# Top-32 attention: no fourth replacement; kept keys found again by signs and a triangle product

## The chip, the cores and the metric

One NeuronCore of one Trainium2 chip runs the whole program. The metric is the device time of one execution in microseconds. The program is a four-layer decoder of twelve sublayers; the change lies in one of them, the self-attention of the last layer.

## The reference, cut to what matters

For each of 8 sequences of 256 tokens and each of 16 heads of 8 features, a query keeps the 32 keys with the highest scores, takes the softmax over these, and mixes their values. Of equal scores the lower key index is kept, since that is how `top_k` orders them.

```python
scores = jnp.einsum('bhsd,bhtd->bhst', q, k) / scale
top_s, top_i = jax.lax.top_k(scores, 32)
probs = jax.nn.softmax(top_s, axis=-1)
v_g = gather(v, top_i)
out = jnp.einsum('bhsk,bhskd->bhsd', probs, v_g)
out = out.transpose(0, 2, 1, 3).reshape(b, s, e)
return out @ Wo.T + bo
```

## The kernel before, in words

`topk_attention` works on 64 groups, one after the other. A group is two heads of one sequence: four tiles (`U = 4`, head by half of the queries) of 128 queries x 256 keys. Two groups share a projected tile of queries and keys, so 32 tiles. Each engine has its own in-order program, and semaphores join them. Nothing is scheduled by a tool: the loops over `t` at the end of each engine's block give the order.

For group n, TensorE writes scores into two PSUM banks (`score`, L3552; two pairs of banks take turns). VectorE (`choose`, L3696 and L3699) then works four rounds: in a round `max` finds the eight highest of each tile, and `match_replace` overwrites exactly these eight (first places first, so ties go right) in the copy `raw`. After four rounds `raw` lacks exactly the 32 kept keys. ScalarE (`soften`) sums the exponentials of the 32 maxima (L3641) and takes exponentials of the scores (L3645) and of `raw` (L3647), whose replaced places give 0. GpSimd (`pick`) subtracts the two (L3747), which leaves the kept keys alone, and multiplies by the inverse sum (L3749). TensorE transposes (`turn`, L3598), ScalarE copies (`take_turned`, L3656), TensorE mixes with the values (`mix`, L3575), ScalarE copies the heads (`take_heads`, L3664). `project` (L3539, L3540) and `take_queries` (L3629, L3630) come once for two groups; `put_out`, `take_output` and `add` once for eight.

Of the kernel before, what the change touches and what calls it, by code (L numbers as in the profile page):

```python
# [70 lines left out]
class Core:  # L71
# [19 lines left out]
        "biases_placed", "mask_spread",  # L91
# [3403 lines left out]
def topk_attention(c):  # L3495
# [6 lines left out]
    NG, GROUPS, TILES = H // 2, B * H // 2, B * H // 4  # L3502
    a = Arena(c)
    qb, kb = a.take(2, S), a.take(2, S)
    probs, rest, raw = a.take(2, U, S), a.take(2, U, S), a.take(2, U, S)
# [3 lines left out]
    nbias, sums, rsum = a.take(2, U), a.take(2, U), a.take(2, U)  # L3509
    top8, few = a.take(2, U, K // 8, 8), a.take(2, U, K)  # L3510
    values = c.T[:, 0, :].rearrange("p (t f) -> p t f", f=P)
# [6 lines left out]
    def scores(n):  # L3518
        return c.psum[:, 2 * (n % 2):2 * (n % 2) + 2, :].rearrange("p a (q k) -> p (a q) k", k=S)
# [10 lines left out]
    with nc.Block() as block:  # L3530
        @block.tensor
        def _(pe):
# [10 lines left out]
            def score(n):  # L3543
                tile = n // 2
                if n % 2 == 0:
                    pe.wait_ge(c.qk_taken.sem, c.qk_taken.at(tile + 1))
                if n >= 2:
                    pe.wait_ge(c.probs_ready.sem, c.probs_ready.at(n - 1))
                for u in range(U):
                    lo = (n % 2 * 2 + u // 2) * 32  # L3550
                    head = slice(lo, lo + 32)
                    mm = nc.tensor.matmul(scores(n)[:, u, :], qb[head, tile % 2, u % 2 * P:(u % 2 + 1) * P],  # L3552
                                          kb[head, tile % 2, :], start=True, stop=True, tile_position=(lo, 0))
                mm.then_inc(c.scores_ready.sem, 1)
# [9 lines left out]

            def mix(n):
                b, tile = n // NG, n // 2
                pe.wait_ge(c.turned_copied.sem, c.turned_copied.at(n + 1))
                if n == 0:
                    pe.wait_ge(c.v_taken.sem, c.v_taken.at(4))
# [18 lines left out]
            def turn(n):  # L3588
                pe.wait_ge(c.probs_picked.sem, c.probs_picked.at(n + 1))
                if n == 0:  # L3590
                    pe.wait_ge(c.v_taken.sem, c.v_taken.at(4))
                else:
                    pe.wait_ge(c.turned_copied.sem, c.turned_copied.at(n))
                for head in range(2):
                    for kt in range(2):
                        for q in range(2):
                            at = (kt * 2 + q) * P
                            mm = nc.tensor.transpose(bank(4 + head)[:, at:at + P],  # L3598
                                                     probs[:, n % 2, 2 * head + q, kt * P:(kt + 1) * P], ident)
                mm.then_inc(c.probs_turned.sem, 1)  # L3600
# [6 lines left out]
            for t in range(GROUPS + 3):  # L3607
                if t + 1 < GROUPS:
                    score(t + 1)
                if t % 2 == 0 and t // 2 + 1 < TILES:  # L3610
                    project(t // 2 + 1)
# [6 lines left out]
                if 0 <= t - 1 < GROUPS:  # L3618
                    turn(t - 1)

        @block.scalar
        def _(act):
            ch = Chain(act, c.scalar_chain)

            def take_queries(tile):
                act.wait_ge(c.qk_ready.sem, c.qk_ready.at(tile + 1))
                if tile >= 2:
                    act.wait_ge(c.scores_ready.sem, c.scores_ready.at(2 * tile - 2))
                nc.scalar.activation(kb[:, tile % 2, :], bank(7)[:, 0:S], ACT.Identity, bias=bk[:, tile % 4:tile % 4 + 1])  # L3629
                nc.scalar.activation(qb[:, tile % 2, :], bank(7)[:, S:2 * S], ACT.Identity,  # L3630
                                     bias=bq[:, tile % 4:tile % 4 + 1]).then_inc(c.qk_taken.sem, 1)

            def soften(n):
                s = n % 2
                act.wait_ge(c.scores_max.sem, c.scores_max.at(n + 1))
                if n >= 2:
                    act.wait_ge(c.sums_inverted.sem, c.sums_inverted.at(n - 1))
                    act.wait_ge(c.probs_turned.sem, c.probs_turned.at(n - 1))
                ch.link(nc.scalar.activation(nbias[:, s, :], top8[:, s, :, 0, 0], ACT.Identity, scale=-SCALE))
                for u in range(U):  # L3640
                    ins = nc.scalar.activation(few[:, s, u, :], top8[:, s, u].rearrange("p r x -> p (r x)"), ACT.Exp,  # L3641
                                               bias=nbias[:, s, u:u + 1], scale=SCALE, accum_out=sums[:, s, u:u + 1])
                ins.then_inc(c.kept_summed.sem, 1)
                for u in range(U):
                    nc.scalar.activation(probs[:, s, u, :], scores(n)[:, u, :], ACT.Exp, bias=nbias[:, s, u:u + 1],  # L3645
                                         scale=SCALE)
                    ins = nc.scalar.activation(rest[:, s, u, :], raw[:, s, u, :], ACT.Exp, bias=nbias[:, s, u:u + 1],  # L3647
                                               scale=SCALE)
                ins.then_inc(c.probs_ready.sem, 1)

# [23 lines left out]
            for t in range(GROUPS + 4):  # L3674
                if 0 <= t - 1 < GROUPS:
                    soften(t - 1)
                if 0 <= t - 2 < GROUPS:
                    take_turned(t - 2)
                if t % 2 == 0 and t // 2 + 1 < TILES:
                    take_queries(t // 2 + 1)  # L3680
                if t % 2 == 1 and 0 <= t - 3 < GROUPS:
                    take_heads((t - 3) // 2)
                if t >= 10 and (t - 10) % NG == 0:
                    take_output((t - 10) // NG)
# [3 lines left out]
        def _(dve):  # L3688
# [3 lines left out]
            def choose(n, r):  # L3692
                src = scores(n) if r == 0 else raw[:, n % 2]
                for u in range(U):
                    ch.all_but(U - 1)
                    ch.step(v.max(top8[:, n % 2, u, r, :], src[:, u, :]))  # L3696
                for u in range(U):
                    ch.all_but(U - 1)
                    ins = v.match_replace(raw[:, n % 2, u, :], top8[:, n % 2, u, r, :], src[:, u, :], REPLACED)  # L3699
                    if r == K // 8 - 1 and u == U - 1:  # L3700
                        ins.then_inc(c.scores_max.sem, 1)
                    else:
                        ch.step(ins)

# [6 lines left out]
            for n in range(GROUPS):  # L3711
                dve.wait_ge(c.scores_ready.sem, c.scores_ready.at(n + 1))
                if n >= 2:
                    dve.wait_ge(c.probs_ready.sem, c.probs_ready.at(n - 1))
                choose(n, 0)
                choose(n, 1)
                if n >= 1:
                    dve.wait_ge(c.kept_summed.sem, c.kept_summed.at(n))
                    if n >= 3:
                        dve.wait_ge(c.probs_picked.sem, c.probs_picked.at(n - 2))  # L3720
                    v.reciprocal(rsum[:, (n - 1) % 2, :], sums[:, (n - 1) % 2, :]).then_inc(c.sums_inverted.sem, 1)  # L3721
# [12 lines left out]
            last = GROUPS - 1  # L3734
            dve.wait_ge(c.kept_summed.sem, c.kept_summed.at(GROUPS))
            dve.wait_ge(c.probs_picked.sem, c.probs_picked.at(GROUPS - 2))
            v.reciprocal(rsum[:, last % 2, :], sums[:, last % 2, :]).then_inc(c.sums_inverted.sem, 1)

        @block.gpsimd
        def _(pool):  # L3740
# [3 lines left out]
            def pick(n):  # L3744
                mine = probs[:, n % 2]
                pool.wait_ge(c.probs_ready.sem, c.probs_ready.at(n + 1))
                ch.link(g.tensor_tensor(mine, mine, rest[:, n % 2], ALU.subtract))  # L3747
                pool.wait_ge(c.sums_inverted.sem, c.sums_inverted.at(n + 1))
                g.tensor_tensor(mine, mine, rsum[:, n % 2, :].unsqueeze(2).broadcast_to([P, U, S]), ALU.mult) \  # L3749
                    .then_inc(c.probs_picked.sem, 1)  # L3750
# [5 lines left out]

            for t in range(GROUPS + 4):
                if 0 <= t - 1 < GROUPS:
                    pick(t - 1)
                if t >= 11 and (t - 11) % NG == 0:  # L3760
                    add((t - 11) // NG)
            ch.clear()
    for s, n in ((c.qk_ready, TILES), (c.qk_taken, TILES), (c.scores_ready, GROUPS), (c.v_ready, 4), (c.v_taken, 4),
                 (c.turned_copied, GROUPS), (c.mixed_ready, GROUPS), (c.out_copied, TILES), (c.out_product, B),
                 (c.probs_turned, GROUPS), (c.scores_max, GROUPS), (c.kept_summed, GROUPS), (c.probs_ready, GROUPS),
                 (c.outputs_kept, B), (c.sums_inverted, GROUPS), (c.probs_picked, GROUPS), (c.out_added, B)):
# [655 lines left out]
```

## Time and profile before

| | |
|---|---|
| median of three runs | 2698.5 us (2695.8 to 2700.4) |
| the profiled execution, its own time | 2686.84 us |
| its span | 2685.0 us |
| mean granted TensorE clock | 0.791 of full speed |
| busy over the span | TensorE 1923.9 us, VectorE 1756.1, ScalarE 1148.4, GpSimd 716.3 |
| the 64 groups of this stage | about 1640 to 2408 us of the span |

Busy time is a sum over the program; the stage is read from windows and timelines inside it. A granted clock of 1.0 is 2.4 GHz, 0.5 is 1.2 GHz; a number between is the mean of a stretch that had both.

### The profile page before, as it was taken

To read this page: it belongs to the slowest core of one execution; us is meant where nothing else is said; L and a number is where in the kernel's file an instruction comes from. 1 tells how busy PE (TensorE), PEld (TensorE's weight loads), DVE (VectorE), ACT (ScalarE), POOL (GpSimd) and SP (SyncE) were. 2 spreads that over 40 slices of the span, in tenths; PEclk is the share of its full clock that TensorE was granted. 3 is DMA by queue.
4 is the path that set the end of the run, shared out by engine and by line. 5 is a ranking of instruction groups with operands and counts; after the bars stand their busy time and mean duration, and the time that the engine had idled before them with its cause. 6 is when DMAs were issued, how large, how long until landed. Compare 5 with 4: busy or idle time off the path is not lost. (4 is left out here: it accounts for less than half of the span.)

```text
span 2685.0 us, 35915 instructions
## 1 busy us (share of the span) xinstructions
PE 1923.9 (72%) x11203; PEld 1116.0 (42%) x11215; DVE 1756.1 (65%) x5569; ACT 1148.4 (43%) x3148; POOL 716.3 (27%) x638
## 2 busy tenths in 40 slices
PE   5996878843877999979986875556555555556777
PEld 1644436422444666644352543333333333324243
DVE  4235322248766666647746567999999999964554
ACT  3553332141314666641233554555555455542312
POOL 1200050405333333310032411333333333331130
PEclk7988889965988999979988887566666566666878
DMA  4000001220000000000100000000000000000000
GB/s 183 2 1 0 25 19 35 47 110 1 2 2 1 1 1 0 0 0 0 77 14 1 1 1 0 1 1 1 1 1 1 0 1 1 1 1 0 0 0 16
DMA packets 10065, 37.04 MB, mean 14 GB/s; under 512 B 1755, under 2 KB 7008, under 8 KB 8752
## 3 DMA queue, kind: packets, MB, share of 16 engines
q1 hardware_dynamic: 7856, 31.69, 3.0%
q0 software_dynamic: 2048, 3.38, 0.6%
q8 instruction: 80, 1.31, 0.2%
q14 instruction: 81, 0.66, 0.1%
HBM read 30.11 MB, written 5.77 MB: 13 GB/s over the span
## 5 line engine op out<-in xcount | busy, mean ns | idle before, releaser
L3552 PE MATMUL psum<-work 32*128 32x256 f32 x512 | 129.9, 652 | 296.8 <-ACT work L3647 296.8
L3699 DVE MATCH_REPLACE8 work<-work 128x256 f32<-128x256 f32 x768 | 306.4, 414 | 0.0
L3747 POOL TENSOR_TENSOR work<-work 128x1024 f32<-128x1024 f32 x64 | 150.7, 2355 | 509.0 <-ACT work L3647 509.0
L3696 DVE MAX8 work<-work 128x8 f32<-128x256 f32 x768 | 267.8, 415 | 0.0
L3552 PEld LDWEIGHTS psum<-work 32*128 32x128 f32 x512 | 77.3, 309 | 323.1 <-ACT work L3647 165.1
L676 POOL TENSOR_TENSOR work<-work 128x256 f32<-128x256 f32 (+2 forms) x144 | 133.3, 944 | 259.3 <-DVE work L936 259.3
L866 ACT ACTIVATE work<-work 128x128 f32<-128x128 f32 (+1 forms) x320 | 144.9, 454 | 38.0 <-PE psum L736 24.6
L337 DVE RECIPROCAL work<-work 128x256 f32<-128x256 f32 x36 | 62.8, 1749 | 123.2 <-ACT work L407 123.0
L3647 ACT ACTIVATE work<-work 128x256 f32<-128x256 f32 x256 | 128.2, 501 | 0.0
L3575 PE MATMUL psum<-work,tiles 128*8 128x256 f32 x512 | 117.0, 610 | 13.8 <-ACT work L3656 13.8
L3749 POOL TENSOR_TENSOR work<-work 128x1024 f32<-128x1024 f32 x64 | 121.1, 1892 | 6.2 <-DVE work L3721 1.2
L3598 PE MATMUL psum<-small_weights,work 128*128 128x128 f32 x512 | 102.7, 367 | 21.6 <-POOL work L3749 21.6
L3645 ACT ACTIVATE work<-psum,work 128x256 f32<-128x256 f32 x256 | 117.5, 459 | 0.0
L3598 PEld LDWEIGHTS psum<-small_weights,work 128*128 128x128 f32 x512 | 84.3, 194 | 70.1 <-POOL work L3749 52.6
L3699 DVE MATCH_REPLACE8 work<-work,psum 128x256 f32<-128x256 f32 x256 | 103.4, 420 | 0.0
L905 DVE CUSTOM_DVE_ANT_0 work<-psum,work 128x128 f32<-128x128 f32 (+1 forms) x320 | 99.6, 368 | 2.8
L3696 DVE MAX8 work<-psum 128x8 f32<-128x256 f32 x256 | 90.9, 421 | 7.2 <-PE psum L3552 5.8
L2080 DVE TENSOR_TENSOR work<-work,psum 128x320 f32<-128x320 f32 (+1 forms) x56 | 32.1, 574 | 88.4 <-PE psum L1951 88.4
L832 ACT ACTIVATE work<-psum,big_weights 128x256 f32<-128x256 f32 x128 | 57.8, 474 | 73.2 <-PE psum L722 72.8
L796 PE MATMUL psum<-work 128*64 128x256 f32 (+2 forms) x640 | 72.7, 346 | 19.6 <-DVE work L931 19.6
L736 PE MATMUL psum<-small_weights,work 128*128 128x128 f32 x512 | 83.5, 281 | 3.7 <-POOL work L676 3.7
L270 PE MATMUL psum<-residual,small_weights 128*128 128x512 f32 x96 | 58.5, 741 | 38.7 <-PEq L189 22.8
(597 smaller groups left out, 4682.0 us busy)
## 6 DMA issues: line engine op xcount, KB each, us to landing
big_weights<-L0f_dram SPq DMA_DIRECT2D x1, 6053.5 KB, 25.8
big_weights<-L_dram SPq DMA_DIRECT2D x1, 5892.0 KB, 16.6
big_weights<-L_dram SPq DMA_DIRECT2D x1, 4952.5 KB, 15.7
big_weights<-L_dram SPq DMA_DIRECT2D x1, 2091.0 KB, 20.2
big_weights<-L_dram SPq DMA_DIRECT2D x1, 1630.5 KB, 11.8
big_weights<-L0f_dram SPq DMA_DIRECT2D x1, 1630.5 KB, 6.4
slots_in<-tiles SPq DMA_DIRECT2D x1, 1280.0 KB, 9.4
residual<-x_dram SPq DMA_DIRECT2D x1, 1024.0 KB, 4.9
```

The lines of the kernel that those rows point to most:

```text
L676: ins = nc.gpsimd.tensor_tensor(part, part, rsum[:, g % 4, q:U:U // n].unsqueeze(2) .broadcast_to([P, n, seen(q)]), ALU.mult)
L866: ins = nc.scalar.activation(probs[:, g % 2, u, 0:seen(u)], src, ACT.Exp, bias=nbias[:, g % 2, u:u + 1], scale=scale, accum_out=sums[:, g ...
L905: ins = nc.vector.tensor_tensor_reduce(raw[:, s, u, 0:seen(u)], scores(g)[:, u, 0:seen(u)], mask(mb, u % 2)[:, 0:seen(u)], 1.0, NEG, ALU.a ...
L3552: mm = nc.tensor.matmul(scores(n)[:, u, :], qb[head, tile % 2, u % 2 * P:(u % 2 + 1) * P], kb[head, tile % 2, :], start=True, stop=True, t ...
L3575: mm = nc.tensor.matmul(held(tile)[at:at + D, :], values[:, 2 * b + kt, lo:lo + D], turned[:, n % 2, head, kt, :], start=(kt == 0), stop=( ...
L3598: mm = nc.tensor.transpose(bank(4 + head)[:, at:at + P], probs[:, n % 2, 2 * head + q, kt * P:(kt + 1) * P], ident)
L3645: nc.scalar.activation(probs[:, s, u, :], scores(n)[:, u, :], ACT.Exp, bias=nbias[:, s, u:u + 1], scale=SCALE)
L3647: ins = nc.scalar.activation(rest[:, s, u, :], raw[:, s, u, :], ACT.Exp, bias=nbias[:, s, u:u + 1], scale=SCALE)
L3696: ch.step(v.max(top8[:, n % 2, u, r, :], src[:, u, :]))
L3699: ins = v.match_replace(raw[:, n % 2, u, :], top8[:, n % 2, u, r, :], src[:, u, :], REPLACED)
L3747: ch.link(g.tensor_tensor(mine, mine, rest[:, n % 2], ALU.subtract))
L3749: g.tensor_tensor(mine, mine, rsum[:, n % 2, :].unsqueeze(2).broadcast_to([P, U, S]), ALU.mult) \
```

## The change

VectorE does rounds 0, 1 and 2 whole, and of round 3 only the `max`: its four `match_replace` and their value loads go, and so does the second exponential (`rest`). Which keys are kept is worked out anew from the 32nd score:

- TensorE multiplies the scores a second time (`score_again`) into the banks 2 and 3, where before the second pair of score banks was. The scores proper now have one pair for all groups, so `score(n)` waits for the exponentials of n - 1.
- ScalarE (`compare`) takes the sign of (32nd score - score) in bf16 with a row sum: -1 is above, 0 equal, 1 below. TensorE transposes the signs (`turn_signs`), ScalarE squares them (`square`), and TensorE (`rank`) adds up in PSUM, in bf16, -512 times the sign, a row of places, and the squares times a triangle of halves, which counts equal scores ahead. ScalarE makes a positive number of it for kept keys alone (`keep_ranks`), GpSimd clips it to 0 and 1 and multiplies (`pick`).
- The sum of the 32 exponentials is made by one GpSimd subtraction, one exponential and five small GpSimd additions. GpSimd's multiplication by the inverse sum moves to `scale`.
- The orders of the loops change on all engines; small tables are made once on GpSimd.

```diff
-    probs, rest, raw = a.take(2, U, S), a.take(2, U, S), a.take(2, U, S)
+    probs, raw = a.take(2, U, S), a.take(2, U, S)
+    ranks, picked = a.take(U, S), a.take(2, U, S)
...
-    def scores(n):
-        return c.psum[:, 2 * (n % 2):2 * (n % 2) + 2, :].rearrange("p a (q k) -> p (a q) k", k=S)
+    scores = c.psum[:, 0:2, :].rearrange("p a (q k) -> p (a q) k", k=S)
+    order = c.psum[:, 2:4, :].rearrange("p a (q k) -> p (a q) k", k=S)
+    again = order
...
+            def score_again(n):
+                if n:
+                    pe.wait_ge(c.ranks_kept.sem, c.ranks_kept.at(n))
+                multiply_heads(n, again).then_inc(c.scores_again.sem, 1)
...
+            def turn_signs(n):
+                pe.wait_ge(c.signs_ready.sem, c.signs_ready.at(n + 1))
...
+                for kt in range(2):
+                    for u in range(U):
+                        mm = nc.tensor.transpose(signs_t[:, kt, u, :], signs[:, n % 2, u, kt * P:(kt + 1) * P], ident16)
...
+            def rank(n):
+                pe.wait_ge(c.squares_kept.sem, c.squares_kept.at(n + 1))
+                for half in range(2):
...
+                    nc.tensor.matmul(out, far, signs[:, z, 2 * half:2 * half + 2, :].rearrange("p u k -> p (u k)"),
+                                     start=True, stop=False)
+                    for u in (2 * half, 2 * half + 1):
+                        nc.tensor.matmul(order[:, u, :], one_row[0:1, :], place_row[0:1, :], start=False, stop=False)
+                        for kt in range(2):
+                            mm = nc.tensor.matmul(order[:, u, :], squares[:, z, kt, u, :], prefix[:, kt, :], start=False,
...
+            def compare(n):
+                act.wait_ge(c.scores_max.sem, c.scores_max.at(n + 1))
+                act.wait_ge(c.scores_again.sem, c.scores_again.at(n + 1))
...
+                for u in range(U):
+                    ins = nc.scalar.activation(signs[:, s, u, :], again[:, u, :], ACT.Sign, scale=-1.0,
+                                               bias=top8[:, s, u, LAST, 7:8], accum_out=balance[:, s, u:u + 1])
...
+            def keep_ranks(n):
+                act.wait_ge(c.ranks_ready.sem, c.ranks_ready.at(n + 1))
...
+                    ins = nc.scalar.activation(ranks[:, u, :], order[:, u, :], ACT.Relu, scale=2.0,
+                                               bias=balance[:, n % 2, u:u + 1])
...
+                if r == LAST:
+                    return
...
+                ch.link(g.tensor_scalar(ranks, ranks, 1.0, 0.0, ALU.min, ALU.max))
+                g.tensor_tensor(picked[:, n % 2], probs[:, n % 2], ranks, ALU.mult).then_inc(c.probs_picked.sem, 1)
```

On ScalarE a pair of groups before stands as follows (L3639 to L3647 are `soften`, L3656 `take_turned`, L3629 and L3630 `take_queries`, L3664 `take_heads`); the next row after these is the same pattern again.

```order
L3656 COPY work<-psum 128x512
L3629 ACTIVATE work<-psum,big_weights 128x256 [waits scores_ready,qk_ready]
L3630 ACTIVATE work<-psum,big_weights 128x256
L3639 ACTIVATE work<-work 128x4 [waits probs_turned,sums_inverted,scores_max]
L3641 ACTIVATE work<-work 128x32 [waits scalar_chain]
L3641 ACTIVATE work<-work 128x32 x3
```

In the changed program the same engine has, for one step of the loop (L3674 and L3675 `take_queries`, L3732 `take_heads`, L3696 `compare`, L3702 `sum_few`, L3706 `square`, L3683 and L3685 `soften`, L3724 `take_turned`; L3715, `keep_ranks`, follows):

```order
L3674 ACTIVATE work<-psum,big_weights 128x256 [waits scores_again,qk_ready]
L3675 ACTIVATE work<-psum,big_weights 128x256
L3732 COPY work<-psum 128x256 [waits mixed_ready]
L3696 ACTIVATE work<-psum,work 128x256 [waits ranks_ready,scores_again,scores_max]
L3696 ACTIVATE work<-psum,work 128x256 x3
L3702 ACTIVATE work<-work 128x128 [waits centred]
L3706 ACTIVATE work<-psum 128x1024 [waits signs_turned]
L3683 ACTIVATE work<-work 128x4 [waits probs_picked,scores_masked]
L3685 ACTIVATE work<-psum,work 128x256 [waits scalar_chain]
L3685 ACTIVATE work<-psum,work 128x256 x3
L3724 COPY work<-psum 128x512 [waits mixed_ready,probs_turned]
L3724 COPY work<-psum 128x512
```

`take_queries` moved from behind `take_turned` to the head of the step, ahead of `compare`, and ScalarE now waits for something of TensorE's at up to six places of a step (`qk_ready`, `mixed_ready`, `scores_again`, `signs_turned`, `probs_turned`, `ranks_ready`).

On TensorE a step of before is this, in the middle of the stage:

```order
L3552 MATMUL psum<-work 128x256 [waits probs_ready]
L3552 MATMUL psum<-work 128x256 x3
L3539 MATMUL psum<-normed_input,big_weights 128x256 [waits qk_taken]
L3540 MATMUL psum<-normed_input,big_weights 128x256
L3575 MATMUL psum<-work,tiles 8x256 [waits out_copied,turned_copied]
```

And of the change (L3565 is both `score_again`, where it waits for `ranks_kept`, and `score`; L3549 and L3550 `project`, L3589 `turn_signs`, L3637 `turn`, L3597 to L3602 `rank`):

```order
L3565 MATMUL psum<-work 128x256 [waits ranks_kept]
L3565 MATMUL psum<-work 128x256 x3
L3549 MATMUL psum<-normed_input,big_weights 128x256 [waits qk_taken,outputs_kept]
L3550 MATMUL psum<-normed_input,big_weights 128x256
L3589 MATMUL psum<-work 128x128 [waits signs_ready]
L3589 MATMUL psum<-work 128x128 x7
L3637 MATMUL psum<-small_weights,work 128x128 [waits turned_copied,probs_picked]
L3637 MATMUL psum<-small_weights,work 128x128 x7
L3597 MATMUL psum<-work 128x512 [waits squares_kept]
L3600 MATMUL psum<-work 128x256
L3602 MATMUL psum<-work 128x256 x2
```

Behind the rest of `rank` come `score` and `mix`, as before, and then the next `score_again`.

## Rows read from the trace of the kernel before

**Rows 1.** Windows of the stage: PE, PEld, DVE, ACT, POOL busy us, then granted clock.

```profile
2180.00:2240.00 60.00, 32.62 (x136) 18.46 (x137) 59.80 (x252) 31.07 (x104) 21.23 (x10) 0.63 0.00 1
```

**Rows 2.** Timeline, VectorE: start, length, instruction; group 1, two rounds, the last group.

```profile
1655.90 1.42 DVE L3696 MAX8 work<-psum 128x8 f32<-128x256 f32 x4
...
2017.45 1.43 DVE L3696 MAX8 work<-psum 128x8 f32<-128x256 f32 x4 [0.20 <-DVE work L3699]
...
2020.37 1.40 DVE L3696 MAX8 work<-work 128x8 f32<-128x256 f32 x4
...
2390.00 0.43 DVE L3699 MATCH_REPLACE8 work<-work 128x256 f32<-128x256 f32 x1
```

**Rows 3.** Timeline, ScalarE: `soften`, `take_turned`, and an exponential with row sum elsewhere.

```profile
2017.28 0.21 ACT L3639 ACTIVATE work<-work 128x4 f32<-128x4 f32 x1 [2.57 <-DVE work L3699]
2017.52 0.32 ACT L3641 ACTIVATE work<-work 128x32 f32<-128x32 f32 x1
...
2018.75 0.45 ACT L3645 ACTIVATE work<-psum,work 128x256 f32<-128x256 f32 x1
2019.11 0.50 ACT L3647 ACTIVATE work<-work 128x256 f32<-128x256 f32 x1
...
2010.15 1.06 ACT L3656 COPY work<-psum 128x512 f32<-128x512 f32 x2
...
885.25 0.49 ACT L866 ACTIVATE work<-work 128x256 f32<-128x256 f32 x1
...
885.74 0.35 ACT L826 COPY work<-psum 128x256 f32<-128x256 f32 x1
```

**Rows 4.** Groups by line and form: count, busy us, mean ns of one, idle before.

```profile
L1222 ACT ACTIVATE work<-psum 128x1024 f32<-128x1024 f32 x64 | 62.0, 1021 | 42.3 <-PE psum L1129 42.3
L3664 ACT COPY work<-psum 128x256 f32<-128x256 f32 x32 | 11.9, 372 | 96.0 <-PE psum L3575 96.0
L3747 POOL TENSOR_TENSOR work<-work 128x1024 f32<-128x1024 f32 x64 | 150.7, 2355 | 509.0 <-ACT work L3647 509.0
L2602 POOL TENSOR_TENSOR work<-work 128x128 f32<-128x128 f32 x48 | 21.9, 456 | 53.4 <-ACT work L2534 41.6 <-DVE work L2572 10.6 <-DVE work L2569 1.0
L3020 POOL TENSOR_SCALAR tiles<-tiles 128x2048 f32<-128x2048 f32 x1 | 2.2, 2212 | 0.1
```

**Rows 5.** Timeline, TensorE: scores at 2.4 GHz, then a burst at 1.2 GHz, then the last `turn`.

```profile
1642.65 1.14 PE L3552 MATMUL psum<-work 32*128 32x256 f32 x8
...
1975.43 2.08 PE L3552 MATMUL psum<-work 32*128 32x256 f32 x8 [4.13 <-ACT work L3647]
1977.45 1.22 PE L3539 MATMUL psum<-normed_input,big_weights 128*128 128x256 f32 x2
1978.46 1.06 PE L3540 MATMUL psum<-normed_input,big_weights 128*128 128x256 f32 x2
1979.45 1.88 PE L3575 MATMUL psum<-work,tiles 128*8 128x256 f32 x8
1981.27 1.23 PE L3598 MATMUL psum<-small_weights,work 128*128 128x128 f32 x8
...
2387.90 1.97 PE L3598 MATMUL psum<-small_weights,work 128*128 128x128 f32 x8 [1.57 <-POOL work L3749]
```

**Rows 6.** Windows, TensorE alone: busy us and granted clock, this stage and others.

```profile
2010.00:2012.00 2.00, 1.60 (x8) 0.50 0.03 8
2016.00:2018.00 2.00, 0.27 (x3) 1.00 0.00 0
...
1445.00:1460.00 15.00, 11.05 (x25) 0.77 0.00 0
1610.00:1625.00 15.00, 10.05 (x60) 1.00 0.00 0
2475.00:2490.00 15.00, 8.16 (x23) 0.66 0.00 0
```

More of the change, by code:

```diff
@@ L3508, in topk_attention @@
     update = a.take(2, S)
-    nbias, sums, rsum = a.take(2, U), a.take(2, U), a.take(2, U)
+    nbias, sums, rsum, balance = a.take(2, U), a.take(2, U), a.take(2, U), a.take(2, U)
     top8, few = a.take(2, U, K // 8, 8), a.take(2, U, K)
+    ident16, far, place_row, one_row = (a.take(n // 2).bitcast(BF16) for n in (P, P, S, P))
+    prefix = a.take(2, S // 2).bitcast(BF16)
+    strict = a.take(P)
     values = c.T[:, 0, :].rearrange("p (t f) -> p t f", f=P)
@@ L3546, in score, with multiply_heads @@
                     pe.wait_ge(c.qk_taken.sem, c.qk_taken.at(tile + 1))
-                if n >= 2:
-                    pe.wait_ge(c.probs_ready.sem, c.probs_ready.at(n - 1))
+                if n >= 1:
+                    pe.wait_ge(c.probs_ready.sem, c.probs_ready.at(n))
+                multiply_heads(n, scores).then_inc(c.scores_ready.sem, 1)
+            def multiply_heads(n, out):
                 for u in range(U):
@@ L3607, in _ @@
             for t in range(GROUPS + 3):
+                if 0 <= t - 1 < GROUPS:
+                    score_again(t - 1)
+                if t % 2 == 0 and t // 2 + 1 < TILES:
+                    project(t // 2 + 1)
+                if 0 <= t - 1 < GROUPS:
+                    turn_signs(t - 1)
+                if 0 <= t - 2 < GROUPS:
+                    turn(t - 2)
+                if 0 <= t - 1 < GROUPS:
+                    rank(t - 1)
                 if t + 1 < GROUPS:
                     score(t + 1)
-                if t % 2 == 0 and t // 2 + 1 < TILES:
-                    project(t // 2 + 1)
                 if t == 0:
@@ L3640, in soften @@
                 for u in range(U):
[L3641 to L3647, printed above, removed]
+                    ins = nc.scalar.activation(probs[:, s, u, :], scores[:, u, :], ACT.Exp, bias=nbias[:, s, u:u + 1],
@@ L3674, in _ @@
             for t in range(GROUPS + 4):
+                if t % 2 == 0 and t // 2 + 1 < TILES:
+                    take_queries(t // 2 + 1)
+                if t % 2 == 0 and 0 <= t - 4 < GROUPS:
+                    take_heads((t - 4) // 2)
                 if 0 <= t - 1 < GROUPS:
-                    soften(t - 1)
+                    compare(t - 1)
+                    sum_few(t - 1)
+                    square(t - 1)
+                if t >= 11 and (t - 11) % NG == 0:
+                    take_output((t - 11) // NG)
+                if t < GROUPS:
+                    soften(t)
                 if 0 <= t - 2 < GROUPS:
                     take_turned(t - 2)
[L3679 to L3684, printed above, removed]
+                if 0 <= t - 1 < GROUPS:
+                    keep_ranks(t - 1)
             ch.clear()
@@ L3692, in choose @@
             def choose(n, r):
-                src = scores(n) if r == 0 else raw[:, n % 2]
+                src = scores if r == 0 else raw[:, n % 2]
                 for u in range(U):
-                    ch.all_but(U - 1)
-                    ch.step(v.max(top8[:, n % 2, u, r, :], src[:, u, :]))
+                    if r == 1 and u == U - 1:
+                        dve.wait_ge(c.scores_masked.sem, c.scores_masked.at(n + 1))
+                    else:
+                        ch.all_but(U - 2 if r == 1 else U - 1)
+                    ins = v.max(top8[:, n % 2, u, r, :], src[:, u, :])
+                    if r == LAST and u == U - 1:
+                        ins.then_inc(c.scores_max.sem, 1)
+                    else:
+                        ch.step(ins)
+                if r == LAST:
+                    return
                 for u in range(U):
@@ L3717, in _ @@
                 if n >= 1:
[L3718 to L3721, printed above, removed]
+                    invert(n - 1)
                 choose(n, 2)
@@ L3733, in _ @@
                     ch.clear()
[L3734 to L3737, printed above, removed]
+            invert(GROUPS - 1)
         @block.gpsimd
@@ L3742, in _, with tables @@
             g = nc.gpsimd
-            def pick(n):
+            def tables():
+                g.tensor_copy(ident16, ident)
+                g.tensor_scalar(far, ident, -512.0, 0.0, ALU.mult, ALU.add)
+                g.tensor_scalar(place_row, c.w("position"), -1.0, float(K), ALU.mult, ALU.add)
+                g.memset(one_row, 1.0)
+                g.memset(prefix[:, 0, P:], 0.5)
+                g.memset(prefix[:, 1, 0:P], -0.5)
+                ch.link(g.tensor_tensor(strict, c.w("upper"), ident, ALU.subtract))
+                ch.step(g.tensor_scalar(prefix[:, 0, 0:P], strict, 1.0, -0.5, ALU.mult, ALU.add))
+                ch.link(g.tensor_scalar(prefix[:, 1, P:], strict, 1.0, -0.5, ALU.mult, ALU.add))
+                g.memset(strict, 0.0).then_inc(c.tables_ready.sem, 1)
@@ L3755, in add @@
                 g.tensor_tensor(c.X[:, seq], c.X[:, seq], update[:, b % 2, :], ALU.add).then_inc(c.out_added.sem, 1)
+            tables()
             for t in range(GROUPS + 4):
+                if 0 <= t - 2 < GROUPS:
+                    pick(t - 2)
                 if 0 <= t - 1 < GROUPS:
-                    pick(t - 1)
+                    centre_few(t - 1)
+                    add_few(t - 1)
                 if t >= 11 and (t - 11) % NG == 0:
                     add((t - 11) // NG)
+                if 0 <= t - 1 < GROUPS:
+                    scale(t - 1)
             ch.clear()
```

89 lines of the change are left out of this document (69 added, 20 removed).

## The prediction

> **What bounds the kernel now.** The windows come first, since shares of the whole program say nothing of one stage: in 60 us of it VectorE is busy 59.80, ScalarE 31.07, TensorE 32.62, GpSimd 21.23 [rows 1]. VectorE sets the pace. The timeline gives its pitch: from the start of group 1 (1655.90) to the end of the last replacement (2390.43) are 734.5 us for 63 groups, 11.66 us each [rows 2]. A round lasts 2.92 us (2017.45 to 2020.37), of which the four `max` take 1.43, so a round's replacements cost about 1.5 to 1.6 [rows 2]. All else hides behind VectorE: TensorE's scores wait 4.13 us for ScalarE at 1975.43 [rows 5], `soften` waits 2.57 us for VectorE [rows 3].
>
> **What is removed.** The fourth round's replacements: 1.57 us, so VectorE could do a group in 10.1, and the stage would lose 63 x 1.57 = 99 us. That is a floor: VectorE reaches it only if nobody else is slower.
>
> **What is added, and to which loop.** Two chains now go round once a group without passing through VectorE, and the slower of them or VectorE sets the pitch. Prices first.
>
> ScalarE. Exponentials of 256 columns from PSUM follow each other at 0.36 us, the last adds its 0.46 (2018.75, 2019.11) [rows 3]: `keep_ranks` 3 x 0.36 + 0.46 = 1.54, `soften` the same and 0.24 ahead (2017.28 to 2017.52) = 1.78, `take_queries` 0.36 + 0.47 = 0.83. With a row sum a 256-column exponential takes 0.49 to the next instruction (885.25 to 885.74) [rows 3]; from PSUM I take 0.45, so `compare` is 1.9 with its last read. `take_turned` 1.06 [rows 3], `take_heads` 0.37, `square` (1024 columns from PSUM) 1.02 [rows 4]. `sum_few` has 128 columns, between the 0.32 of 32 and the 0.46 of 256: 0.3.
>
> GpSimd. The multiplication in `pick` costs what the subtraction did, 2.36; the clip, one input, is half of 2.21 for 2048 columns, rounded up to 1.2; `centre_few` 0.46 [rows 4].
>
> TensorE, at 1.2 GHz: a score product of four tiles 2.08, a `project` 1.01 + 1.06 = 2.07, `mix` 1.88, `turn` 1.97 [rows 5]. At 2.4 GHz the scores took 1.14 [rows 5], 0.55 of that; I apply 0.55 to all. No row shows `turn_signs` (eight bf16 transposes). Half of `turn`, 1.0, bounds it from below if bf16 needs half the passes, `turn` from above; I take 1.2 (0.65 at 2.4 GHz). `rank` streams 16 passes of 256 columns (two of 512, twelve of 256). The f32 projection has 4 passes of 256 in 1.01 us (1977.45 to 1978.46), 0.253 each, hence 4.05 (2.2 at 2.4 GHz). The tightest row is `mix`, 8 such passes in 1.82 us (1979.45 to 1981.27), 0.228 each, hence 3.6 [rows 5]. Full-height weights as in the projection are nearer; I take 4.05.
>
> The Trainium skill (TensorE: Matmul & The Clock Gate, "Back-to-back issue gap") gives N/1.2 ns for a cold bf16 pass and about N/2.4 for a warm one; an estimate from that page is 3.4 and 1.7 for `rank`. The rows here have 0.253 against its 0.213 per 256 columns.
>
> **Loop one, ScalarE and GpSimd** (`keep_ranks` to the next `keep_ranks`, all in each engine's order). In a step with a projection: scores again 1.14, `project` 1.12, `take_queries` 0.83, `take_heads` 0.37, `compare` 1.9, `turn_signs` 0.65, `square` 1.02, `soften` 1.78, `take_turned` 1.06, `keep_ranks` 1.54: 11.4. In the other the way over GpSimd is longer: clip 1.2, product 2.36, `centre_few` 0.46, `sum_few` 0.3, `square`, `soften`, `take_turned`, `keep_ranks` 5.40: 9.7. With seven handoffs between engines, for which I allow 0.06 each, the mean is (21.1 + 0.4) / 2 = 10.8 us at 2.4 GHz.
>
> **Loop two, TensorE round `compare`**: scores again, `compare`, `turn_signs`, `turn`, `rank`, `score`, `mix`, scores again. At 2.4 GHz 1.14 + 1.9 + 0.65 + 1.08 + 2.2 + 1.14 + 1.03 = 9.1, half a projection with what follows it on ScalarE (1.12 + 0.83 + 0.37) / 2 = 1.2, handoffs 0.2: 10.5. At 1.2 GHz 15.2 + 1.6 + 0.2 = 17.0. If a part x of TensorE's work runs at 1.2 GHz, the pitch is 10.5 + 6.5 x.
>
> So the clock decides. Now this stage has 0.63 [rows 1], and it is ill placed: 0.50 while the burst runs (2010 to 2012), 1.00 when it is over (2016 to 2018, busy 0.27 us) [rows 6]. After the change TensorE has 14.3 us of work per group at 1.2 GHz (2 x 2.08, half of 2.07, 1.2, 1.97, 4.05, 1.88), some 7.9 at 2.4, so it would be busy in 65 to 80% of the time. Windows about so busy elsewhere: 11.05 of 15 us at 0.77, 10.05 at 1.00, 8.16 at 0.66 [rows 6]. With this stage's own 0.63 their mean is 0.77; I take 0.75, because one wait per group stays, that for `compare` (1.9, mean 0.6 for `take_queries` and `take_heads`, handoffs: 2.6 us idle), behind which the clock may fall as now. At 0.75 half the time is at 1.2 GHz, of which 2.6 us find TensorE idle: x = (0.5 T - 2.6) / 14.3. With T = 10.5 + 6.5 x this gives T = 9.32 / 0.773 = 12.06.
>
> **The sum.** 63 x (12.06 - 11.66) = +25 us. The first group ends 1.6 earlier, the last has a longer way from its last maxima to `turn` (`compare`, `turn_signs`, `square`, `rank`, `keep_ranks`, `pick`: 10.9 against some 9 now): +1 together. The tables on GpSimd lie behind VectorE's first group. 2686.84 + 26 = 2713 us for an execution like the profiled one, which lies 11.7 below the median of the runs shown; against these it is 2724.
>
> The edits of memory layout and of `invert` (0.17 us on VectorE, same place in the order) cost nothing while VectorE waits; if VectorE were the bound they would be as dear as now. VectorE's waiting, about 2 us a group, shows at `max` of round 0, for scores held up behind `rank`, and at `invert`. The second exponential's removal (four x 0.4 us) is in the loop sums already, since ScalarE's list is written out.
>
> **Rivals.**
> - *The clock holds* (faster). If TensorE's bursts now follow closely enough for 0.9 or more in this stage, then 0.2 T is less than the 2.6 idle us, x = 0 and loop one bounds: 10.8, 63 x (-0.86) + 1 = -53 us, 2646. It decides from a granted clock of 0.78 up, where T = 11.66. For it: 1.00 at 10.05 of 15 us busy [rows 6]. Against it: 0.77 at 11.05, and the wait for `compare`.
> - *The clock stays as it is*, 0.62: x = (0.76 T - 2.6) / 14.3, T = 14.2, +161 us, 2860. For it: the same alternation of burst and idle time. Against it: a group's contiguous stretch from `turn_signs` to the next scores is over twice as long.
> - *`rank` is cheaper*: at the 0.228 of `mix`, loop two is 10.3 + 6.3 x over 13.9 us of work, T = 11.8, +9 us; with a clock of 0.77 it is no change. By the page's gap, at 0.75, the estimate is 11.5 and -12 us.
> - *VectorE stays the bound* at 10.1: -98 us, 2600. It needs both loops half a us and more shorter than their rows, which no row supports.
>
> **How the numbers follow.** The forecast (clock 0.70 to 0.78, pitch 11.75 to 13) 0.45; the clock near 0.62, 0.15; the clock holds 0.27; VectorE bound 0.03; no change (clock about 0.78, or a cheaper `rank`) 0.10. A measurement of this kernel tells 0.2%, 5 us, from no change. Faster 0.30, same 0.10, slower 0.60. The range goes down to the case of the held clock, 2646, and up to a clock of 0.68 (T = 13.15, +95 us), rounded to 2800; below lies some 0.05, above some 0.13. The likeliest case alone has 2705 to 2784.
>
> **What would show it.** Right: 12.0 us between the first `max` of neighbouring groups; VectorE busy under 90% in the stage; a granted clock there of 0.7 to 0.78; ScalarE idle ahead of `square` for TensorE, and ahead of `compare` for the second scores; `rank` at about 4 us at 0.5 and 2.2 at 1.0; GpSimd some 7.5 us a group. Wrong: a clock of 0.8 or more with less than 11.5 us a group; `rank` clearly below 3.6 us cold; `compare` far from 1.9; scores ready before VectorE asks for them in every group.

## The result, and the profile after

The changed kernel takes 2818.2 us (median of 4, 2814.1 to 2820.4) against 2699.2 for the kernel before on the same chip: a ratio of 1.0441, 95% interval 1.0423 to 1.0459. It is slower, as forecast, but by 119 us instead of 26, and it lies above the range.

The windows of the stage in the changed kernel (columns as in [rows 1]); the second is the window of one stretch inside it:

```profile
1660.00:2500.00 840.00, 650.53 (x3405) 344.61 (x3468) 631.39 (x2524) 479.14 (x1378) 417.92 (x554) 0.71 0.00 1
2000.00:2060.00 60.00, 46.23 (x248) 25.38 (x253) 44.33 (x180) 35.86 (x105) 31.09 (x43) 0.73 0.00 1
```

VectorE is busy 631 of 840 us, 75%; before it was 99.7% [rows 1]. The most used engine is now TensorE, 650.5 us, 77%, at a granted clock of 0.71. The timeline of VectorE gives the pitch:

```profile
2008.16 1.43 DVE L3773 MAX8 work<-psum 128x8 f32<-128x256 f32 x4 [0.95 <-PE psum L3565]
...
2022.51 1.43 DVE L3773 MAX8 work<-psum 128x8 f32<-128x256 f32 x4 [2.17 <-PE psum L3565]
...
2510.53 1.42 DVE L3773 MAX8 work<-psum 128x8 f32<-128x256 f32 x4
```

The step between the first two lasts 14.35 us, the one ahead of it 12.9 and the one behind it 13.6. From the start of group 1 (1667.7) to that of the last group (2510.5) the mean is 13.59 us, where before it was 11.66 [rows 2]: 63 x 1.93 = 122 us, 3 more than the medians differ by. From the first `max` of the stage to the end of the span the two traces differ by 119.0 us; the other 13.4 us of the difference of their spans arise far ahead of the stage (the last section). VectorE waits where the prediction said, at the first `max` for scores (L3565), and at `invert` (L3792). The waits of 1700 to 2400, some 52 groups (who waited for whom; us in total, times, longest; `issue` is idle time for which the profile shows no releaser):

```profile
PE psum L3589 <- ACT work L3696: 133.1, 52, 3.0
...
ACT work L3696 <- issue: 118.9, 25, 6.1
DVE work L3792 <- POOL work L3854: 103.1, 52, 3.5
DVE work L3773 <- PE psum L3565: 72.3, 45, 2.2
ACT work L3715 <- PE psum L3602: 71.1, 45, 1.9
ACT work L3674 <- PE psum L3550: 67.1, 26, 2.6
```

TensorE waits once a group, in every group, for the signs of `compare` (L3696), 2.6 us on average. ScalarE waits for `rank` (L3602) in 45 of the 52 groups, and in each second group for `project` (L3550); in the others it stands idle ahead of `compare`, which starts when the second scores are through (2028.12 in the trace, the scores of 2026.87 below). That is loop two, TensorE round `compare`. What the clock does to it is seen in one step of TensorE's timeline, and in the windows of the same microseconds (busy times in the order of [rows 1], then the clock):

```profile
2009.00 1.14 PE L3565 MATMUL psum<-work 32*128 32x256 f32 x8
2010.07 0.70 PE L3549 MATMUL psum<-normed_input,big_weights 128*128 128x256 f32 x2
2010.61 0.59 PE L3550 MATMUL psum<-normed_input,big_weights 128*128 128x256 f32 x2
2014.23 0.62 PE L3589 MATMUL psum<-work 128*128 128x128 bf16 x8 [3.02 <-ACT work L3696]
2014.68 1.13 PE L3637 MATMUL psum<-small_weights,work 128*128 128x128 f32 x8
...
2018.09 0.63 PE L3597 MATMUL psum<-work 128*128 128x512 bf16 x1
...
2020.37 2.08 PE L3565 MATMUL psum<-work 32*128 32x256 f32 x8
2022.38 1.88 PE L3614 MATMUL psum<-work,tiles 128*8 128x256 f32 x8
2024.19 2.75 PE L3623 MATMUL psum<-work,big_weights 128*128 128x256 f32 x8
2026.87 1.14 PE L3565 MATMUL psum<-work 32*128 32x256 f32 x8
```

```profile
2010.00:2014.00 4.00, 1.20 (x6) 0.68 (x4) 4.00 (x17) 2.76 (x11) 2.62 (x2) 1.00 0.00 0
2014.00:2016.00 2.00, 1.59 (x16) 1.31 (x17) 0.07 (x2) 1.49 (x5) 1.19 (x5) 0.88 0.00 0
2016.00:2018.00 2.00, 1.50 (x6) 0.65 (x8) 2.00 (x9) 1.97 (x7) 1.69 (x1) 0.50 0.00 0
2018.00:2024.00 6.00, 6.00 (x25) 2.08 (x23) 3.83 (x15) 2.13 (x6) 1.92 (x3) 0.50 0.01 3
```

While TensorE waits (2010 to 2014, busy 1.20 of 4 us) the granted clock is 1.00. It falls only as `turn` comes to its end, and so `rank`, the scores, `mix` and the first part of `put_out` run at 1.2 GHz (the 2.75 us of `put_out` at a mean clock of 0.72): a scores product of four tiles takes 1.14 us at 2009.00 and 2.08 at 2020.37. In this step the idle time stands at 2.4 GHz and the work behind it at 1.2. It isn't so in every step: the wait ahead of this one, 2.09 us up to 2001.11, stands at 1.2 GHz. Over all groups 1.31 of 3.05 us of idle time a group are at 1.2 GHz, and 6.56 of 10.54 us of busy time.

### The profile page after: what moved, and what is told of

It is laid out like the page before. It is cut to its first block and busy times, and to the rows that moved or that the text cites. A ratio compares the mean times of both kernels' runs of the same rounds, so it can differ in the third digit from the quotient of the medians.

```text
span 2817.4 us, 40074 instructions
## 1 busy us (share of the span) xinstructions
PE 2177.7 (77%) x13059; PEld 1235.9 (44%) x13135; DVE 1666.0 (59%) x5057; ACT 1258.5 (45%) x3276; POOL 883.8 (31%) x1096
## 5 line engine op out<-in xcount | busy, mean ns | idle before, releaser
L3782 DVE MATCH_REPLACE8 work<-work 128x256 f32<-128x256 f32 x512 | 203.6, 409 | 0.0
L3565 PE MATMUL psum<-work 32*128 32x256 f32 x1024 | 199.9, 521 | 4.6 <-ACT work L3685 3.9
L3696 ACT ACTIVATE work<-psum,work 128x256 bf16<-128x256 f32 x256 | 118.4, 483 | 154.1 <-issue 144.0
L3589 PE MATMUL psum<-work 128*128 128x128 bf16 x512 | 50.8, 258 | 161.7 <-ACT work L3696 161.7
L3565 PEld LDWEIGHTS psum<-work 32*128 32x128 f32 x1024 | 118.8, 245 | 72.6 <-issue 41.4
L3715 ACT ACTIVATE work<-psum,work 128x256 f32<-128x256 f32 x256 | 100.6, 480 | 90.4 <-PE psum L3602 90.4
L3866 POOL TENSOR_SCALAR work<-work 128x1024 f32<-128x1024 f32 x64 | 66.5, 1039 | 226.8 <-issue 218.2
L3602 PE MATMUL psum<-work 128*128 128x256 bf16 x512 | 131.9, 351 | 0.0
L3589 PEld LDWEIGHTS psum<-work 128*128 128x128 bf16 x512 | 37.3, 115 | 195.2 <-ACT work L3696 195.2
L3852 POOL TENSOR_TENSOR work<-work 128x64 f32<-128x64 f32 (+3 forms) x256 | 63.5, 248 | 167.6 <-ACT work L3702 152.5
L3600 PE MATMUL psum<-work 1*128 1x256 bf16 x256 | 88.3, 345 | 32.3 <-ACT work L3706 19.0
L3685 ACT ACTIVATE work<-psum,work 128x256 f32<-128x256 f32 x256 | 100.3, 474 | 2.1
```

The costliest lines, as they stand in the source:

```text
L3565: mm = nc.tensor.matmul(out[:, u, :], qb[head, n // 2 % 2, u % 2 * P:(u % 2 + 1) * P], kb[head, n // 2 % 2, :], start=True, stop=True, til ...
L3602: mm = nc.tensor.matmul(order[:, u, :], squares[:, z, kt, u, :], prefix[:, kt, :], start=False, stop=(kt == 1 and u % 2 == 1))
L3685: ins = nc.scalar.activation(probs[:, s, u, :], scores[:, u, :], ACT.Exp, bias=nbias[:, s, u:u + 1], scale=SCALE)
L3696: ins = nc.scalar.activation(signs[:, s, u, :], again[:, u, :], ACT.Sign, scale=-1.0, bias=top8[:, s, u, LAST, 7:8], accum_out=balance[:, ...
L3715: ins = nc.scalar.activation(ranks[:, u, :], order[:, u, :], ACT.Relu, scale=2.0, bias=balance[:, n % 2, u:u + 1])
```

## The experiments

All are compared with the kernel before, run on the same chip; there its median was 2694.9 us for e1 to e4, 2685.1 for e5 to e8 and 2699.8 for e9 and e10, so the ratios are to be compared, not the medians. Pitch, granted clock and x (the part of TensorE's work done at 1.2 GHz) are my sums over each trace's records, from the first `max` of group 1 to that of the last group; the last column is the prediction's formula for loop two, 10.5 + 6.5 x, for the kernels whose loops are those of the changed one.

| kernel | us, median | ratio, 95% interval | pitch | clock | x | 10.5 + 6.5 x |
|---|---|---|---|---|---|---|
| before | 2699.2 | 1 | 11.66 | 0.62 | 0.82 | |
| changed | 2818.2 | 1.0441 [1.0423, 1.0459] | 13.59 | 0.71 | 0.47 | 13.6 |
| e1_fill | 2647.7 | 0.9823 [0.9807, 0.9840] | 10.93 | 0.99 | 0.01 | 10.6 |
| e2_clip_twice | 2844.1 | 1.0545 [1.0507, 1.0583] | 13.99 | 0.68 | 0.54 | 14.0 |
| e3_replace_back | 2810.2 | 1.0429 [1.0412, 1.0447] | 13.43 | 0.73 | 0.46 | 13.5 |
| e4_mix_in_wait | 2653.8 | 0.9876 [0.9827, 0.9925] | 10.97 | 0.91 | 0.12 | |
| e5_mix_queries | 2602.5 | 0.9688 [0.9672, 0.9704] | 10.40 | 0.93 | 0.10 | |
| e6_fill3 | 2646.3 | 0.9861 [0.9832, 0.9891] | 11.12 | 0.87 | 0.18 | |
| e7_few_late | 2626.7 | 0.9791 [0.9766, 0.9817] | 10.59 | 0.95 | 0.07 | |
| e8_before_fill | 2684.3 | 0.9998 [0.9987, 1.0008] | 11.66 | 0.79 | | |
| e9_few_late_no_fill | 2658.3 | 0.9853 [0.9836, 0.9869] | 10.98 | 0.84 | 0.22 | |
| e10_fill2 | 2807.4 | 1.0398 [1.0381, 1.0416] | 13.59 | 0.71 | 0.47 | 13.6 |

Theory one: the pitch is loop two's, and TensorE's clock sets it. The rivals: loop one (ScalarE and GpSimd) is longer than I thought and the clock only keeps it company; or VectorE's waits at `invert` matter.

**e1_fill.** Six products whose results nobody uses, where TensorE waits for the signs.

```diff
+            def fill(count):
+                for _ in range(count):
+                    nc.tensor.matmul(bank(4), ident16, prefix.rearrange("p t q -> p (t q)"), start=True, stop=True)
...
+                if 2 <= t and t - 1 < GROUPS:
+                    fill(6)
                 if 0 <= t - 1 < GROUPS:
                     turn_signs(t - 1)
```

> The changed kernel with six extra bf16 products of 512 columns on TensorE (into a bank that nobody reads then) while it waits for `compare`. Theory one, the loop through TensorE sets the pitch and half of it runs at 1.2 GHz: the granted clock of the stage rises from 0.71 to 0.9 or more, the pitch falls from 13.6 to 10.8 to 11.5 us a group, the whole to 2640 to 2690 us. Rival, ScalarE and GpSimd set the pitch: the clock may rise, the time stays within 1% of 2818. Second rival, more work on TensorE simply lengthens its loop: 2830 to 2900.

The window of e1_fill, and TensorE's timeline with the filler (L3571, 1.46 us) and `rank` behind it:

```profile
1660.00:2300.00 640.00, 552.15 (x3626) 293.97 (x3628) 594.55 (x2395) 456.62 (x1310) 397.09 (x526) 0.98 0.00 1
```

```profile
2008.59 1.46 PE L3571 MATMUL psum<-work 128*128 128x512 bf16 x6
2011.78 0.62 PE L3593 MATMUL psum<-work 128*128 128x128 bf16 x8 [1.73 <-ACT work L3702]
2012.24 1.04 PE L3641 MATMUL psum<-small_weights,work 128*128 128x128 f32 x8
...
2014.81 0.38 PE L3601 MATMUL psum<-work 128*128 128x512 bf16 x1
...
2016.19 1.14 PE L3565 MATMUL psum<-work 32*128 32x256 f32 x8
```

About half of the wait is filled (TensorE's idle time falls from 3.05 to 1.46 us a group), it has more to do than in the changed kernel, and the clock is 0.98: the kernel becomes 5.9% faster than the changed one (0.9823 / 1.0441) and 1.8% faster than the one before. The clock is the cause of the loss. The pitch of 10.93 leaves loop one 10.9 at most; the prediction had 10.8.

**e2_clip_twice.** GpSimd's clip, done twice (the values are the same).

```diff
                 ch.link(g.tensor_scalar(ranks, ranks, 1.0, 0.0, ALU.min, ALU.max))
+                ch.link(g.tensor_scalar(ranks, ranks, 1.0, 0.0, ALU.min, ALU.max))
```

> The changed kernel with GpSimd's clip of the ranks done twice (1.04 us and a handoff more a group). Theory one, the loop through TensorE: no change, 2813 to 2825, as long as the picked keys are still ready when `turn` is due. Rival, the loop through ScalarE and GpSimd sets the pitch: 0.5 to 1.1 us a group more, 2850 to 2888.

2844.1 lies above the first range and below the rival's: neither forecast holds, and the time alone doesn't decide. The steps do. From group 28 on they are those of the changed kernel to 0.02 us (12.84, 14.35, 12.89, 14.35), with 1.04 us more on GpSimd in each; it comes out of GpSimd's wait ahead of its small additions (L3852), 37.3 us in 29 groups where the changed kernel has 72.7 in 30 (2000 to 2400). The loss lies ahead of group 23, which ran in another order of clock levels, with steps of 12.3 to 17.9 us. With its x of 0.54 the formula gives the 14.0 measured. That GpSimd's time stands in the pitch is refuted for these groups; what put the first groups into the other order stays open.

**e3_replace_back.** VectorE does the fourth round's replacements again, behind its last maxima, for nobody.

```diff
                 if r == LAST:
+                    for u in range(U):
+                        ...
+                        ch.step(v.match_replace(raw[:, n % 2, u, :], top8[:, n % 2, u, r, :], src[:, u, :], REPLACED))
                     return
```

> The changed kernel with the fourth round's replacements done again on VectorE, behind its last maxima (their result is not used). Theory one: VectorE has over 3 us a group to spare, so 2813 to 2830. Rival, VectorE's own work is still in the pitch: 1.57 us a group more, near 2915.

```profile
1660.00:2500.00 840.00, 675.44 (x3532) 347.57 (x3532) 735.96 (x3061) 486.99 (x1398) 426.33 (x565) 0.72 0.00 1
```

VectorE is busy 735.96 of 840 us now, 105 more, and the pitch is 13.43, not longer. VectorE has slack; its waits at `invert` cost nothing.

**e4_mix_in_wait and e5_mix_queries.** The work of TensorE that hurries nobody goes into the wait for the signs, and ScalarE's copies out from ahead of `compare`.

```diff
+                if 0 <= t - 3 < GROUPS:
+                    mix(t - 3)
                 if 0 <= t - 1 < GROUPS:
                     turn_signs(t - 1)
...
-                if 0 <= t - 2 < GROUPS:
-                    mix(t - 2)
```

On ScalarE, in e4 `take_heads` moves behind `square`, and in e5 `take_queries` too:

```diff
-                if t % 2 == 0 and t // 2 + 1 < TILES:
-                    take_queries(t // 2 + 1)
                 if 0 <= t - 1 < GROUPS:
                     compare(t - 1)
                     sum_few(t - 1)
                     square(t - 1)
+                if t % 2 == 0 and t // 2 + 1 < TILES:
+                    take_queries(t // 2 + 1)
```

> The changed kernel with `mix` moved on TensorE from behind `score` to behind the next `score_again` and `project`, into the wait for `compare`, and `take_heads` moved behind `square` on ScalarE. Theory one: `mix` leaves the loop, 1.0 us at 2.4 GHz and 1.9 at 1.2, and `take_heads` 0.37 in every other group: pitch 11.5 to 12.5, 2685 to 2750 us. Rival, ScalarE and GpSimd set the pitch: only `take_heads`'s share, 2800 to 2818.

> The kernel with `mix` in the wait, and `take_queries` moved on ScalarE behind `square`, so that `compare` no longer waits for the projection (1.1 us at 2.4 GHz, 2.1 at 1.2, and 0.83 on ScalarE, every other group). Theory one, the loop from `keep_ranks` over the second scores, now the bound at 10.97 us: it loses about 1 us a group in the mean and VectorE's 10.1 comes in sight: 2600 to 2635 us. Rival, the loop over GpSimd's `pick` sets the pitch: at most 10 us less than 2654.

The windows of e5:

```profile
1660.00:2300.00 640.00, 520.28 (x3440) 295.86 (x3500) 621.74 (x2521) 482.92 (x1392) 426.67 (x561) 0.93 0.00 1
2000.00:2060.00 60.00, 49.35 (x332) 28.17 (x336) 59.87 (x245) 46.02 (x133) 41.26 (x55) 0.94 0.00 1
```

e4 did better than its figure: the clock rose too, to 0.91, which the figure had left out. How much of the gain is the shorter loop and how much the clock was not separated. In e5 VectorE is busy 59.87 of 60 us in the second window: there it is the bound again. Four steps in eight last 10.05 us, which confirms the floor of 10.1. This version beats both kernels: 3.1% faster than before, 7.2% than the changed one (0.9688 / 1.0441).

**e6_fill3, e7_few_late, e9_few_late_no_fill.** e6 is e5 with three filler products between `mix` and `turn_signs`. e7 is e6 with `sum_few` behind `square` on ScalarE. e9 has that move without the filler.

```diff
                     compare(t - 1)
-                    sum_few(t - 1)
                     square(t - 1)
+                    sum_few(t - 1)
```

> The former kernel with three extra bf16 products of 512 columns on TensorE ahead of `turn_signs`. Theory one: the granted clock of the stage goes to 0.95 or more, pitch 10.2 to 10.6, 2600 to 2620 us. Rival, the clock is no longer in the pitch once TensorE's loop is short: same time as the kernel without them, within 5 us.

> The former kernel with `sum_few` behind `square` on ScalarE, so that `square` no longer waits for GpSimd's `pick` and `centre_few`. Theory one: the loop over GpSimd goes, VectorE's 10.1 us is the pitch, 2597 to 2610 us. Rival: `invert`, which now comes later, holds VectorE up by as much, no change or up to 20 us more.

> The version with mixing and take_queries moved, and now sum_few behind square on ScalarE as well, without any filler products. Theory one (with the clock up, TensorE has little in the way and the loop through ScalarE and GpSimd sits just above VectorE's 10.1 us): taking sum_few (about 0.5 us with its wait) out from between compare and square lets the odd steps end earlier; pitch 10.1 to 10.4 against the 10.40 without the move, so 2585 to 2605 us, ratio 0.963 to 0.969. Rival: the wait for centre_few's result simply moves behind square, and delays soften and thereby keep_ranks by as much as it freed; then no change or a few us slower, 2600 to 2620. The 20 us that the same move brought with the filler in place would then belong to the filler.

All three missed. The windows of e6, of e7, and of two stretches of e9:

```profile
1660.00:2300.00 640.00, 560.29 (x3373) 301.59 (x3429) 583.12 (x2350) 452.46 (x1293) 395.81 (x521) 0.87 0.00 1
```

```profile
1660.00:2300.00 640.00, 542.56 (x3544) 296.24 (x3605) 610.98 (x2475) 472.56 (x1368) 416.32 (x552) 0.95 0.00 1
```

```profile
2000.00:2060.00 60.00, 52.04 (x305) 29.11 (x309) 53.38 (x218) 40.72 (x120) 37.65 (x49) 0.80 0.01 1
2200.00:2260.00 60.00, 47.42 (x338) 26.92 (x340) 59.48 (x243) 46.17 (x135) 41.28 (x55) 1.00 0.00 1
```

The four combinations by ratio and clock: neither 0.9688 (0.93), filler 0.9861 (0.87), `sum_few` late 0.9853 (0.84), both 0.9791 (0.95). Each edit alone costs 1.7 to 1.8%, and either takes back part of what the other cost. So neither has a price of its own. e9 shows why in one run: its program is the same in both stretches, yet at 0.80 VectorE is busy 53.4 of 60 us, and at 1.00 it is 59.5, with steps of 10.05 us. So the move doesn't hold VectorE up where the clock is 1.00; the loss goes with the groups at the lower clock. That the clock makes them slow, and not the reverse, is shown by e1 and e10 for the changed kernel, and only argued for this one. Why one order of the same work is granted more than another isn't settled. In e6 a part is direct: ScalarE waits up to 1.9 us for `turn_signs` (L3593), which now stands behind the filler (1700 to 2300; the same wait of e5 below it):

```profile
ACT work L3712 <- PE psum L3593: 53.9, 37, 1.9
ACT work L3706 <- PE psum L3589: 10.3, 16, 2.6
```

**e8_before_fill.** The kernel before, with six products of 256 columns in f32 ahead of `turn`.

> The kernel before the change with six extra f32 products of 256 columns on TensorE ahead of `turn`, where it is idle. Theory one: the granted clock of the stage rises from 0.62, but VectorE sets the pitch of 11.66, so no change, 2690 to 2705 us. Rival, a faster TensorE is worth something there too: below 2685.

The window of the kernel before, and then that of e8:

```profile
1656.00:2390.00 734.00, 411.35 (x1672) 230.67 (x1672) 732.56 (x3086) 383.98 (x1283) 272.38 (x133) 0.62 0.00 1
1656.00:2390.00 734.00, 522.67 (x2403) 342.48 (x2400) 729.94 (x3075) 384.38 (x1289) 271.89 (x133) 0.79 0.00 1
```

The clock of the stage rises from 0.62 to 0.79, and the time stays (0.9998). The median of 2684.3 falls below the 2685 of the rival only because this chip ran the kernel before in 2685.1. Where VectorE bounds, TensorE's clock is worth nothing.

**e10_fill2.** Two filler products where e1 had six.

> The changed kernel with two filler products (512 columns, bf16, results unused) ahead of turn_signs, where the first experiment had six. Theory one says that the pitch follows the share x of TensorE's work at 1.2 GHz, 10.5 + 6.5 x plus at most what filler spills over; whatever granted clock comes out, the pitch goes with it: at 0.75 about 12.9 us, at 0.85 about 11.8, at 0.95 about 10.9. I expect the clock between the changed kernel's 0.71 and the 0.98 of six products, near 0.80, pitch 12.4, about 2745 us, range 2660 to 2815. Rival, that the six products helped because they delay turn_signs and so shift the order of the loops, not by the clock: then two products give about a third of the gain at an unchanged clock of 0.71, 2760 us. The clock column tells them apart, not the time.

```profile
1660.00:2500.00 840.00, 688.28 (x3531) 352.12 (x3594) 631.69 (x2525) 480.26 (x1380) 418.41 (x555) 0.71 0.00 1
```

Near 0.80 and 2745 us were expected, and both were missed: the clock didn't rise, and the steps are those of the changed kernel to 0.02 us from group 12 on. So the effect isn't in proportion: two products gave none, six nearly all. The rival, that the filler helps by shifting `turn_signs`, wanted 2760 and falls too, since clock and pitch stayed together. By the ratio the median is 0.4% below the changed kernel's. The profiled execution, at 2818.3 us, isn't: the other three took 2805.8 to 2807.7; the last section names a candidate.

## Why the prediction was right or wrong

*The floor and what was removed*: right. VectorE can do a group in 10.05 us (e5) where 10.1 was said, and has slack in the changed kernel (e3).

*Loop two, 10.5 + 6.5 x*: right, to 0.1 us in the changed kernel, e2, e3 and e10, at x from 0.46 to 0.54. That it is so exact is in part luck, since errors of its terms cancel. `rank` was priced too low: its second half takes from 2018.09 to 2020.37, 2.28 us, so 4.6 in all at 1.2 GHz against 4.05, and in e1 from 2014.81 to 2016.19, so 2.8 at 2.4 GHz against 2.2. Its estimate by the Trainium skill (TensorE: Matmul & The Clock Gate, "Back-to-back issue gap"), 3.4 and 1.7, is farther off: the page gives that gap for a product by itself, and the measurement decides against it as the price of such a mixed row of passes, with one-row weights among them. `turn_signs` was priced too high, 0.45 us to the next instruction at 2.4 GHz (2014.23 to 2014.68) against 0.65 and 0.82 at 1.2 GHz against 1.2, and so were `take_queries` and `take_heads`, 0.98 us together (2011.24 to 2012.22) against 1.20. `compare` was right, 1.9 (2028.12 to 2030.04). `put_out`, 2.75 us in one group of eight at a clock of 0.72, was left out: 0.3 a group.

*The first and the last group*: the +1 us of the sum doesn't follow from its own terms, which give 0.3 (1.9 longer at the end, 1.6 shorter at the start). In the traces the first step is 1.6 us shorter (13.5 against 15.1), and from the last group's first `max` to the end of the span it is 0.6 longer.

*Loop one, 10.8*: consistent with e1's 10.93; that it is this loop which bounds there, and not loop two at 10.6, no run tells.

*The clock: the step that failed.* "x = (0.5 T - 2.6) / 14.3" holds two choices, and both fell on the cheap side.

- "2.6 us find TensorE idle" at 1.2 GHz. It is idle 3.05 us a group, but only 1.31 of them are at 1.2 GHz. The argument was that the clock falls behind the wait as it did before; it falls later, on the work (2016 to 2024 above). With 1.31 of idle time at 1.2 GHz and the rest as predicted, T is 12.82 instead of 12.06: +0.76 us.
- "I take 0.75", the mean of windows from other stages and this one. It is 0.71, so 0.58 of the time is at 1.2 GHz. With that alone T is 12.64: +0.58 us.

Both together give 13.44 of the 13.59 measured, so 63 x 1.38 = 87 of the 93 us missed are this term; the 0.15 left is less than the 0.3 of `put_out`. x was 0.24 in the prediction and is 0.47. Why the clock fell on the work and not in the wait, and why its mean was 0.71, stays open.

*The rivals.* "The clock holds" gives 2646. e1 with its clock of 0.98 is this case, with 2647.7, or 2651 by its ratio to the 2699.2 of the first chip; it needed filler. "The clock stays as it is": 14.2 at x 0.57; the changed kernel lies nearer to this one (0.6 us away) than to the forecast (1.5), and it deserved more than 0.15. "`rank` is cheaper": refuted; and its price rested on a misreading of [rows 5]. The eight rows of `mix` run in pairs that start within 0.01 us of each other (in the trace before at 1979.455 and 1979.462, the next at 1979.843), so 0.228 us is no time of one pass among passes in line. "VectorE stays the bound" at 2600: not in the changed kernel, but nearly in e5, whose pitch is 10.40; its 2602.5 is from the chip where the kernel before took 2685.1, and is 2615 by its ratio to 2699.2. The condition, both loops clearly shorter, was nearly met by reordering alone.

*What would show it*: 12.0 us between first `max`, wrong (13.59); VectorE under 90%, right (75%); clock 0.70 to 0.78, right by its lower end; ScalarE idle ahead of `square` for TensorE, right, 0.5 to 0.9 us; ahead of `compare`, right; `rank` about 4 us, 4.6; GpSimd some 7.5 us a group, 6.8 (417.92 us in 61.8 groups).

## What to carry to other kernels

A work item that leaves a saturated engine for TensorE must be priced at the clock that the new arrangement is granted, and the question is not only the mean clock but which work stands at 1.2 GHz: in this case 6.6 of the 10.5 busy us a group did, and only 1.3 of the 3.05 idle ones. With the measured mean clock alone the prediction's sum gives 62 us more than before; with this placing too, 112. Where a loop runs through TensorE with a wait in each round, move work that hurries nobody into the wait first (e4 and e5: 5.4 and 7.2% faster than the changed kernel); filler is the test of whether the clock is the cause (e1), and it cost 1.8% where the loop was tight (e6). Where another engine is saturated, the clock is worth nothing (e8).

## What the runs showed of the hardware

- The granted clock and the program's loop fall into one repeating row of steps. In the changed kernel the steps repeat every eight groups to 0.02 us (12.84, 14.35, 12.88, 14.35, 12.92, 14.35, 13.62, 13.93), and e2 and e10, with 1 us more on GpSimd or 0.6 us more on TensorE in each group, come to the same row. So an edit can be free, or shift all groups to another row (e2 ahead of group 23; e9, which changed rows on its way). Differences of 1 to 2% between orders of the same work may be this alone (e5, e6 and e9 fit it; that no other cost is in them wasn't shown).
- The program ahead of the stage is the same in all kernels, and yet VectorE's first `max` of the stage comes at 1640.8 us before and 1654.2 after. Up to 501 us of the span the two traces agree to 0.3 us; then, in the changed kernel's, ScalarE stands idle once for 28.2 us, with VectorE and TensorE behind it. The profile gives no instruction of this program as the releaser, it calls it `remote`. The waits of 498 to 532 in the changed kernel's trace (the trace of before has none for `remote`), and the windows of 500 to 530, before and after:

```profile
ACT work L1982 <- remote: 28.2, 1, 28.2
DVE work L2081 <- ACT work L1982: 27.4, 1, 27.4
...
PE psum L1951 <- DVE work L2081: 21.7, 1, 21.7
```

```profile
500.00:530.00 30.00, 23.02 (x92) 13.71 (x91) 7.39 (x11) 3.58 (x6) 19.45 (x20) 0.90 0.31 46
500.00:530.00 30.00, 8.62 (x32) 4.45 (x30) 1.69 (x3) 1.69 (x3) 19.14 (x20) 0.73 0.29 44
```

- The traces fall in two groups by this wait. Those of e5, e6, e7, e8 and the kernel before don't have it, and the stage comes at 1636 to 1644 us. Those of e1, e2, e3, e4, e9, e10 and the changed kernel have a wait for `remote` of 24 to 28 us (the longest of each) at the same place, on ScalarE, VectorE or both, and the stage comes at 1648 to 1654. The kernel before took 2686.8 us in its profiled execution, without the wait, and 2695.8 to 2700.4 in the others. So this wait may be what separates the chips' medians of the kernel before, and e10's three shorter executions from its profiled one; that wasn't shown, nor was what the wait is for.
